# Gather and put-back products that alternate between the two batches of a pair, in a fused attention and routed-FFN kernel

## What is computed

```python
x = _layernorm(x + _L0_attn_ref(...), axis=-1)
x = _layernorm(x + _L0_ffn_ref(...), axis=-1)
```

## Time and profile before

| | |
|---|---|
| runs | 831.65, 834.04, 833.54 us; median 833.54 |
| profiled execution | span 830.0 us from its first to its last instruction; its own total is not given, the median of the runs is 3.5 us above the span |
| busy: PE, PEld | 678.9 us (82%), 401.4 us (48%) |
| busy: DVE, ACT, POOL | 595.4 us (72%), 554.2 us (67%), 392.0 us (47%) |
| instructions | 16995, of them 6576 matmuls |
| chain that ended last | PE 61%, DVE 18%, issue 10%, ACT 7%, POOL 3% |
| mean granted TensorE clock | 0.828 |
| DMA | 36.75 MB, mean 44 GB/s |

### The profile page before, as it was taken

How to read it: one execution, slowest core, us unless ns; L and a number is a source line. 1 busy time by engine, 2 the same in 40 slices (tenths; PEclk the granted TensorE clock), 3 DMA queues, 4 the chain that set the end, 5 groups by cost and what they waited for, 6 DMA issues and landing times.

```text
span 830.0 us, 16995 instructions
## 1 busy us (share of the span) xinstructions
PE 678.9 (82%) x6576; PEld 401.4 (48%) x6576; DVE 595.4 (72%) x1681; ACT 554.2 (67%) x403; POOL 392.0 (47%) x399
## 2 busy tenths in 40 slices
PE   3588787889979988999899988998899879865652
PEld 2344334455546455645455545645565535434232
DVE  4442718777787788958888788769896986588455
ACT  0588688889768876959768876788687968600000
POOL 5263436447544574346455664446546543421201
PEclk8567678899789987989789987899799979985755
DMA  6321302033300503030304030120303030000001
GB/s 190 64 42 37 64 13 53 25 61 119 64 14 17 112 12 67 27 64 14 64 14 90 14 64 15 50 54 2 64 26 65 2 64 27 13 1 26 0 0 51
DMA packets 96913, 36.75 MB, mean 44 GB/s; under 512 B 68018, under 2 KB 94146, under 8 KB 96834
## 3 DMA queue, kind: packets, MB, share of 16 engines
q1 hardware_dynamic: 96834, 35.67, 18.8%
HBM read 14.69 MB, written 4.19 MB: 23 GB/s over the span
## 4 chain that ended last, share of the span: by engine, by line
PE 61%; DVE 18%; issue 10%; ACT 7%; POOL 3%; DMA 1%; POOLq 0%; DVEq 0%; ACTq 0%
PE ps_y L1199 16%; PE ps_s L1182 14%; ACT pr L731 4%; PE ps_m L1308 3%; PE ps_m L1230 3%; ACT th L716 3%; PE ps_m L1206 3%; PE ps_a L1230 3%; PE ps_m L1356 2%; PE ps_a L1393 2%; DVE v_aug L844 2%; PE ps_m L1258 2%; PE ps_a L1206 2%; PE ps_a L1258 1%; PE ps_a L1292 1%
## 5 line engine op out<-in xcount | busy, mean ns | idle before, releaser
L716 ACT ACTIVATE th<-ps_s 128x1024 f32<-128x1024 f32 (+1 forms) x256 | 280.2, 1129 | 110.7 <-PE ps_s L1182 102.0
L627 POOL TENSOR_TENSOR pr<-pr,tri 128x320 f32<-128x320 f32 (+1 forms) x256 | 194.8, 784 | 186.7 <-ACT pr L731 186.7
L731 ACT ACTIVATE pr<-th 128x2304 f32<-128x2304 f32 x128 | 271.5, 2122 | 15.5 <-PE ps_y L1199 15.4
L1182 PE MATMUL ps_s<-q_st,k_st 32*64 32x512 f16 (+7 forms) x2048 | 193.1, 319 | 24.9 <-ACT th L716 20.8
L1199 PE MATMUL ps_y<-pr,v_aug 128*32 128x512 f32 (+7 forms) x2048 | 157.4, 439 | 0.4 <-POOL pr L627 0.4
L1182 PEld LDWEIGHTS ps_s<-q_st,k_st 32*64 32x64 f16 x2048 | 92.3, 114 | 120.0 <-issue 54.3
L1199 PEld LDWEIGHTS ps_y<-pr,v_aug 128*32 128x32 f32 x2048 | 57.0, 113 | 66.9 <-issue 47.4
L641 POOL TENSOR_TENSOR st<-qk,st 128x1024 f16<-128x1024 f32 x32 | 73.8, 2327 | 32.3 <-DVE st L860 32.3
L629 POOL TENSOR_TENSOR k_wide<-qkT,head_of 128x1024 f32<-128x1024 f32 x16 | 30.1, 1902 | 58.0 <-DVE qkT L1029 58.0
L629 POOL TENSOR_TENSOR r<-x,rw_row 128x512 f32<-128x512 f32 x16 | 18.9, 1180 | 63.6 <-DVE x L922 63.6
L702 ACT ACTIVATE hq<-hu 128x512 f32<-128x512 f32 x8 | 5.0, 630 | 60.7 <-POOL hu L629 60.7
(11 more groups left out here) (220 smaller groups left out, 1133.9 us busy)
## 6 DMA issues: line engine op xcount, KB each, us to landing
x_in<-in_L_attn_x SPq DMA_DIRECT2D x16, 256.0 KB, 2.8
x_res<-in_L_attn_x SPq DMA_DIRECT2D x16, 256.0 KB, 3.1
result<-y_out SPq DMA_DIRECT2D x16, 256.0 KB, 2.4
mask_a<-in_L_ffn_attention_mask SPq DMA_DIRECT2D x3, 1024.0 KB, 5.2
pr<-in_L_ffn_attention_mask SPq DMA_DIRECT2D x2, 1024.0 KB, 8.6
w_sb<-in_L_ffn_w SPq DMA_DIRECT2D x2, 256.0 KB
q_st<-st SPq DMA_TRANSPOSE x16, 4.5
k_st<-st SPq DMA_TRANSPOSE x16, 4.7
```

The source lines that it names most:

```text
L627: return nc.gpsimd.tensor_tensor(buf, buf, tri[:, None, :].to_broadcast([P, blocks, 64]), ALU.mult)
L716: nc.scalar.activation(th[:, gi % 2, c0:c1], ps_s[:, c0:c1], ACT.Tanh, scale=1.0 / (QK_SCALE ** 2 * DH ** 0.5 * SOFTCAP))\
L731: nc.scalar.activation(pr[:, probs_at(n):probs_at(n) + GROUP], th[:, gi % 2, :], ACT.Exp, scale=SOFTCAP).then_inc(exp_done, 1)
L1182: last = mm(ps_s[64 * s:64 * s + 64, COL[kb]:COL[kb] + S - 64 * kb], k_st[rows, k, gi // 2, 64 * kb:64 * kb + 64], q_st[rows, k, gi // 2, ...
```

## The change

Gather and put-back become one step each, in which the batches alternate inside c. The 16 angle columns are copied once behind the 129 columns of `x1` (both batches' buffers, five copies in the first five batches), so that one product gives all 145 columns; the last copies stay valid, since all later batches use the same angles. The gather waits for both `E` and for the copies. The put-back waits for both banks ahead of its first product and raises one signal behind its last. `late.z0` and `late.z1` both wait for that signal. In `PE_ORDER` the second gather entry is left empty. The reserve for software DMA descriptors is made smaller, which frees memory for the wider `x1`.

```diff
-    "late": ["w2", "sc0", "sc1"],
+    "late": ["w2", "sc"],
...
-    ["sel.gather@-1"], ["sel.gather1@-1"],
-    [], ["fin.yT/0@0", "late.sc0@-2", "late.sc1@-2", "fin.wo/0@0", "pv.0/1@0"],
+    ["sel.gather@-1"], [],
+    [], ["fin.yT/0@0", "late.sc@-2", "fin.wo/0@0", "pv.0/1@0"],
...
-        x1 = sb("x1", [P, 2, NT, D + 1])
+        x1 = sb("x1", [P, 2, NT, D + 1 + 2 * DH])
...
+                if b.no < TRIG_COPIES:
+                    row = NT * min(b.no, MASKS - 1)
+                    nc.vector.tensor_copy(x1[:, k, :, D + 1:], trig[:, row:row + NT, :]).then_inc(trig_in_place, 1)
...
             def late_sc(q, k):
-                pe["late"].wait(v, q, f"sc{k}")
+                pe["late"].wait(v, q, "sc")
...
-            def sel_gather(q, k):
-                ve["route"].wait(t_, Batch(q, k), "E")
-                if k == 0:
-                    bank_free("sel.gather", q)
-                rows = slice(SLOTS * k, SLOTS * k + SLOTS)
+            def sel_gather(q, _):
+                for k in range(2):
+                    ve["route"].wait(t_, Batch(q, k), "E")
+                t_.wait_ge(trig_in_place, min(2 * q + 2, TRIG_COPIES))
+                bank_free("sel.gather", q)
                 for c in range(NT):
-                    mm(at("sel.gather")[rows, 0:D + 1], E[:, c, rows], x1[:, k, c, :], start=(c == 0), stop=(c == NT - 1))
-                for c in range(NT):
-                    last = mm(at("sel.gather")[rows, D + 1:D + 1 + 2 * DH], E[:, c, rows],
-                              trig[:, NT * trig_row(Batch(q, k)) + c, :], start=(c == 0), stop=(c == NT - 1))
-                if k == 1:
-                    pe["sel"].done(last, "gather", q)
+                    for k in range(2):
+                        rows = slice(SLOTS * k, SLOTS * k + SLOTS)
+                        last = mm(at("sel.gather")[rows, 0:D + 1 + 2 * DH], E[:, c, rows], x1[:, k, c, :],
+                                  start=(c == 0), stop=(c == NT - 1), skip_group_check=True)
+                pe["sel"].done(last, "gather", q)
...
-            def late_sc(q, k):
+            def late_sc(q, _):
                 ve["late"].wait(t_, q, "proc")
-                bank_free(f"late.sc{k}", q)
-                rows = slice(SLOTS * k, SLOTS * k + SLOTS)
+                bank_free("late.sc0", q)
+                bank_free("late.sc1", q)
                 for c in range(NT):
-                    last = mm(at(f"late.sc{k}")[:, P * c:P * c + P], ET[rows, P * c:P * c + P], proc[rows, :], start=True, stop=True)
-                pe["late"].done(last, f"sc{k}", q)
+                    for k in range(2):
+                        rows = slice(SLOTS * k, SLOTS * k + SLOTS)
+                        last = mm(at(f"late.sc{k}")[:, P * c:P * c + P], ET[rows, P * c:P * c + P], proc[rows, :],
+                                  start=True, stop=True)
+                pe["late"].done(last, "sc", q)
...
+TRIG_COPIES = MASKS + 1
...
-    nc = _bacc.Bacc("TRN2", target_bir_lowering=False, num_devices=1)
+    nc = _bacc.Bacc("TRN2", target_bir_lowering=False, num_devices=1, dynamic_dma_scratch_size=4096)
```

More of the change, by code:

```diff
@@ L467, in build @@
         gate_ready = sem("gate_ready")
+        trig_in_place = sem("trig_in_place")
         turned = [sem(f"turned{i}") for i in range(2)]
@@ L988, in _ @@
             sel_ET = copy_step("sel", "ET", lambda: nc.vector.tensor_copy(ET[:, :], at("sel.ET")[:, :]),
-                               [(pe["late"], lambda q: q - 1, "sc1")])
+                               [(pe["late"], lambda q: q - 1, "sc")])
             sel_R = copy_step("sel", "R", lambda: nc.vector.tensor_copy(R[:, :], at("sel.R")[:, :]),
@@ L1281, in route_thr @@
                 pe["route"].done(tr(at("route.thr", b)[:, 0:P], cand.to_broadcast([P, P]), ident[:, :]), "thr", b)
-            def trig_row(b):
-                return min(b.no, MASKS - 1) if isinstance(b.no, int) else MASKS - 1
-            def sel_gather(q, k):
-                ve["route"].wait(t_, Batch(q, k), "E")
-                if k == 0:
-                    bank_free("sel.gather", q)
-                rows = slice(SLOTS * k, SLOTS * k + SLOTS)
-                for c in range(NT):
-                    mm(at("sel.gather")[rows, 0:D + 1], E[:, c, rows], x1[:, k, c, :], start=(c == 0), stop=(c == NT - 1))
-                for c in range(NT):
-                    last = mm(at("sel.gather")[rows, D + 1:D + 1 + 2 * DH], E[:, c, rows],
-                              trig[:, NT * trig_row(Batch(q, k)) + c, :], start=(c == 0), stop=(c == NT - 1))
-                if k == 1:
-                    pe["sel"].done(last, "gather", q)
+            def sel_gather(q, _):
[3 more added lines that the diff above has]
+                bank_free("sel.gather", q)
+                for c in range(NT):
+                    for k in range(2):
[3 more added lines that the diff above has]
+                pe["sel"].done(last, "gather", q)
             def sel_ET(q, _):
@@ L1415, in _ @@
                      "fin.y0T": lambda b, k: fin_y(b, 0, k), "fin.y1T": lambda b, k: fin_y(b, 1, k),
-                     "fin.yT": fin_yT, "fin.wo": fin_wo, "route.wrow": route_wrow, "route.won": route_won, "route.thr": route_thr, "sel.gather": lambda q, _: sel_gather(q, 0), "sel.gather1": lambda q, _: sel_gather(q, 1),
+                     "fin.yT": fin_yT, "fin.wo": fin_wo, "route.wrow": route_wrow, "route.won": route_won, "route.thr": route_thr, "sel.gather": sel_gather,
                      "sel.ET": sel_ET, **{f"sel.R{c or ''}": (lambda q, _, c=c: sel_R(q, c)) for c in range(NT)}, "sel.RT": sel_RT, "sel.hnT": sel_hnT, "sel.qkv": sel_qkv,
@@ L1421, in _ @@
                      "att.h2T": att_h2T, "att.w1": att_w1, "late.w2": late_w2,
-                     "late.sc0": lambda q, _: late_sc(q, 0), "late.sc1": lambda q, _: late_sc(q, 1)}
+                     "late.sc": late_sc}
             def body(p):
```

## The result

The median went from 833.7 us (831.65 to 834.04, four runs) to 860.38 us (857.33 to 860.69, four runs): a ratio of 1.0318, with an interval from 1.0298 to 1.0337. The change costs 26.7 us. I had forecast 842.6, in a range up to 853: the sign is right, the size lies outside. The profiled execution, the shortest of the four, took 857.33 us, with a span of 855.5.

The account below looks back on a forecast made before the run. VectorE and ScalarE were taken to bound the kernel ahead of Y, TensorE behind it. Terms - 1.9 + 5.9 - 0.2 + 0.3 + 5 = + 9.1 gave 839.1 us of span, 842.6 as median; range 829 to 853.

Parts of the forecast that it names:

- who paces Y: From the copy of v to Y, VectorE and ScalarE set the pace and TensorE waits (1.11 us at the third put-back).
- Y: The end of VectorE's copy of yT, which the put-back's second half waited for; it starts 0.10 us behind.
- Rival C: TensorE's work counts wherever it stands, so its savings reach the end: 817.2 us; chance 0.15 with its milder form, 830.
- the added waits for tanh: Behind the shorter gather, the two later score halves wait for ScalarE's tanh, so the transposes of y come hardly sooner.
- the gather's and the put-back's mechanism: Gather: 16 instructions in 1.1 us, 1.8 less a pair. Put-back: all 16 start at Y + 0.10, alternate, take about 1.14.
- rival D: The put-back's pairs do not overlap; 16 instructions take 2.1 us, w_o another 1.0 later, six times: 848.6 us; chance 0.03.
- The wait ahead of w_o: Behind the joint put-back, w_o waits for VectorE's late z0: 0.8 + 4 x 1.06 + 0.9 = 5.9 us lost.
- The 1.9 us that I counted as won by the gather: At gathers where VectorE waited for rows: about 0.5 at the first, 0.4 at the second, 1.0 at the eighth.
- the clock's term: New clock falls behind four put-backs that had full clock; mean price 3.95 us, a third counted: 5 us lost.
- my sum: All terms added to the profiled span of 830.0 us: - 1.9 + 5.9 - 0.2 + 0.3 + 5 = + 9.1.
- The small terms: 0.2 us won at the eighth put-back, where z1 comes sooner; 0.3 us lost for VectorE's five angle copies.
- B: The clock falls at all four put-backs that had full clock behind Y: + 4.1 + 4 x 3.95, 853 us; chance 0.12.

Follow-up runs that it names:

- the put-back filled: Kernel before with only the joint, alternating put-back, plus its first half's products made once more in bank a ahead of the wait for bank m: 836.33 us, 1.0046.
- the table above: Kernel before, put-back 0's products twice. Gather in two entries: 828.79 in order, 833.27 alternating and made three times; in one entry: 860.96 and 849.54 us.
- the short gather in two entries: New gather made once, eight instructions on either side of the score half, with the old put-back, its first half made twice: 858.57 us, 1.0308.
- the gather only: Kernel before with the new gather and its angle columns, the put-back kept in two steps: 855.11 us, 1.0274.
- The halves: Kernel before with one part of the change each: new gather with old put-back, 855.11 us; old gather with new put-back, 859.94 us.
- one filler: Put-back 0's products made twice: in the kernel before, 828.79 us; in the kernel with the new gather three times and the old put-back, 849.54 against 839.87.
- both fillers: Whole change, gather products three times and put-back 0's once more: 850.59 us; also with value products ahead of w_o, 846.38, or the gather parted, 850.47.
- the alternating kernel in one entry: New gather made three times in one list entry, with the old put-back, its first half made twice: 849.54 us, 1.0210.

## Why the prediction was right or wrong

**Right: who paces Y.** "Ahead of Y, VectorE and ScalarE set the pace and TensorE waits": in five of six put-backs Y comes as long behind v as before (within 0.3 us), though TensorE works 14 us less there. Rival C, 817 us (its terms add up to -16.4, not -16.3), fell with it. Only at the third put-back is Y 1.4 us later; the added waits for tanh appeared where I put them.

**Right: the gather's and the put-back's mechanism.** 16 instructions in 1.21 us (I said 1.2 at most); put-back pairs 0.01 to 0.04 us apart, and the 16 of them done in 1.16 us where the clock was full (I said 1.14), so rival D is out. The wait ahead of w_o has VectorE's addition as its releaser, in these waits of after (185 to 740 us: total, times, longest):

```profile
PE ps_s L1186 <- ACT th L717: 10.5, 12, 1.8
...
PE ps_a L1262 <- DVE sel_v L809: 6.0, 6, 1.1
```

Six times, 6.0 us. Its terms, 0.8 at the first put-back, 1.06 at the middle ones and 0.9 at the sixth, measured 0.77, 1.03 and 0.91 in the put-back filled. The Trainium skill (TensorEngine Tiling (Array Packing), Gotcha 1: PSUM Pressure) says that row tiles write to different banks and that software has to synchronise them. The row of six waits agrees. The 1.9 us that I counted as won by the gather can't be found. VectorE's waits for the gathered rows are gone, but at the first gather Y came at 175.29 us instead of 175.33, and at the second 0.15 us later behind v than before.

**Wrong: the clock's term.** The step that failed reads "A fall ahead of Y is partly spent idle, where it costs nothing, so I count a third of the four: 5 us". What the runs show in its place: low clock reaches behind Y at all six put-backs, and at the first gather, which I hadn't counted. The falls do begin ahead of Y (2.5 to 3.6 us of low clock there), and part of that is idle. But the low stretches reach another 6.6 to 7.8 us behind Y, where TensorE sets the pace. Against the former 11.0, the stretches at 14.7 to 15.2 lose 3.7 to 4.2, of which 1.0 is the wait. The four put-backs that had full clock lost 3.94, 4.06, 3.98 and 3.52 us; the two that had a fall before changed by -0.67 and +0.52. Taking off the wait (0.77, 1.03 or 0.91), a new fall is worth 2.6 to 3.2, or some 0.41 us for each low microsecond behind Y, less than my mean of 3.95. Of the 15.4 us behind Y, six waits are then 5.8 and the clock 9.5, where I had 5. So the price of a fall was too high and the count, a third of four, much too low.

That is 4.5 of the 16.4 us by which the span's growth (25.5) exceeds my sum (9.1). The rest I had at nothing or with the wrong sign: 5.9 of added waiting between the masks and the next v, whose cause stays open; 2.2 of low clock behind the first gather; 1.9 for the gain that did not come; 1.5 from v to Y, nearly all of it at the third; and 0.5 that I can't place. The small terms make -0.1.

Of the rivals, B ("the clock falls at all four") was the one that happened. That its 853 is short by only 7 is partly luck: its clock term, 4 x 3.95 = 15.8, was too high by 6.3 and hid as much of the missing stretches. The Trainium skill (TensorE: Matmul & The Clock Gate, Part 1) says that idleness brings the throttle back; the falls in all four agree with it. I had that outcome in the text and gave it 0.12.

**In no term: the place.** I expected the waits for tanh that come with the emptied second gather entry, and costed them at nothing. By the table above the emptied entry alone can cost 16 to 32 us where put-back 0 is made twice. What it costs in the change itself is not shown: with the short gather in two entries (858.57) the time is no better than that of the gather only in one (855.11).

**What the sum couldn't have.** The halves cost 21.9 and 26.7 and both together 26.7, and one filler gains in one kernel and loses in another. So effects on the clock may not be added part by part.

**Open.** Why the kernels with both fillers stay at 846 to 851, although three of six put-backs of one of them have full clock, at 12.02 to 12.06; why put-back 0 made twice costs 9.7 us behind the gather made three times; why two products ahead of the wait for `hn` bring more falls; and which measure of TensorE's work the chip goes by. A rival that no run separates: every edit also shifts when TensorE works and when it waits, and the put-back filled came out at 834 to 842 or at 852 to 855 with one program, so part of what the fillers gain or lose may be that shift and not the length of the idle time. What is shown is that taking work away ahead of Y, in either half of the change, is followed by low clock behind it, and that putting as much back into the same half took most or all of the loss away (855.11 to 839.87, and 859.94 to 836.33).

## What to carry to other kernels

Where TensorE is 90% busy on average but waits for others in one stretch, work taken from it there becomes idle time, and its price may be paid in the next stretch, where TensorE is the bound at a lower clock. Ask ahead of such a change which levels of the clock the next stretch shows now, and whether two stretches that look alike already differ: that is a kernel on the edge, in which a small edit can tip several stretches at once. A repeated product in a wait ahead of a TensorE-bound stretch is a cheap trial (828.8 against 832.9 here), but measure it, since the same trick in another wait cost 17 us, and the very same one in another version of this kernel 9.7.

## What the runs showed of the hardware that I had not expected

- More TensorE work can be faster: 839.87 with the gather made three times against 855.11 with it once; 833.27 against 858.57 in another pair.
- Falls of the clock repeat at one spacing: in the alternating kernel in one entry they begin at 260.8, 352.9, 445.1, 537.2 and 629.4 us, 92.1 to 92.2 apart, though Y came 91.3 to 92.6 us apart.
- Alternating the gather's two column halves in f32 made it 1.45 times faster (1.76 to 1.21 us for 16 instructions of 145 columns).
- One program can come out at two times: the put-back filled took 833.91 to 841.64 us in six executions and 851.99 to 855.31 in three.
